# One TensorE signal per slot in a hand-scheduled vision tower kernel

## The reference, cut to what matters

```python
# tok: 256 patches of 16 pixels, mean, layer norm, attention over the 16 pixels
kv = _ln(unf, ln_kv_w, ln_kv_b) @ Wkv.T
h1 = reduce_feats + softmax(q * scale . k) . v @ proj_w.T + proj_b
# attn: gated scan over 256 tokens, forward and backward, 16 states
h = exp(delta * A) * h + delta * u * B ;  y = h . C + D * u
h2 = h1 + (sigmoid(gate(mean y)) * y * silu(z)) @ W_out
# ffn: product keys, 8 heads; the best 16 of 64x64 rows of a table per token and head
sim = einsum(q, pk_keys); scores, idx = top_k(sim, 16)       # twice
final_scores, pk_idx = top_k(score, 16)                      # of the 16x16 pairs
k, v = weighted sums of keys_table, values_table rows        # one per token
out = h2 + sum over heads of causal_softmax(q k^T) v @ Wo
```

## Time and profile before

| | us |
|---|---|
| median of three runs (lowest, highest) | 17585.84 (17570.04, 17600.08) |
| profiled execution: span | 17612.8 |
| one image: span / 64 | 275.2 |
| PE, ACT, DVE, POOL busy | 13397.9, 7416.4, 10470.6, 10063.1 |

### The profile page before, as it was taken

The page is one execution under the profiler, slowest core; times in us unless marked ns, Lnnn a source line. Parts: engine busy times, 40 slices in busy tenths (PEclk is TensorE's granted clock), DMA queues, the critical chain, the costliest instruction groups (busy, mean ns, idle before and its releaser), DMA issues.

```text
span 17612.8 us, 261382 instructions
## 1 busy us (share of the span) xinstructions
PE 13397.9 (76%) x71228; PEld 10390.9 (59%) x71228; DVE 10470.6 (59%) x39940; ACT 7416.4 (42%) x17286; POOL 10063.1 (57%) x9220
## 2 busy tenths in 40 slices
PE   4777777777777777777777778777777777777777
PEld 3656556556565555565656656556556665565565
DVE  6656656566566566565665656656656566566562
ACT  2444444444444444444444444444444444344443
POOL 2555555556556556555555556555655555556565
PEclk6888888888888888888888888888888788788888
DMA  2444434444444344343443444444434444344343
GB/s 80 115 114 113 114 108 115 118 110 119 114 112 118 108 115 122 107 116 109 116 117 107 118 111 120 117 113 116 116 108 117 115 112 116 105 116 122 107 116 95
DMA packets 1643030, 1984.06 MB, mean 113 GB/s; under 512 B 527806, under 2 KB 1129022, under 8 KB 1628990
## 3 DMA queue, kind: packets, MB, share of 16 engines
q1 hardware_dynamic: 1346366, 1359.69, 27.2%
q0 software_dynamic: 294912, 604.57, 13.2%
HBM read 1898.00 MB, written 65.01 MB: 111 GB/s over the span
## 4 chain that ended last, share of the span: by engine, by line
PE 38%; another core or an unknown queue 20%; DVE 15%; issue 13%; ACT 8%; DMA 4%; SPq 1%; DVEq 0%; ACTq 0%
PE bank L890 9%; PE bank L926 6%; DMA moving<-keyspace 4%; PE bank L913 4%; ACT bank L1158 3%; PE bank L907 3%; PE bank L767 2%; PE bank L814 2%; PE bank L875 2%; ACT weight L1164 2%; PE bank L896 1%; PE bank L949 1%; PE bank L851 1%; DVE decay L1484 1%
## 5 line engine op out<-in xcount | busy, mean ns | idle before, releaser
L695 POOL DMA_INDIRECT gath<-in_table_dram,rowsT x9216 | 10062.9, 1092 | 7503.4 <-PE bank L926 3775.8
L890 PE MATMUL bank<-weight,rowtab 128*128 128x256 f32 x12288 | 3919.7, 450 | 0.0
L1164 ACT ACTIVATE weight<-bank 128x512 f32<-128x512 f32 x3584 | 2129.3, 594 | 2782.6 <-PE bank L913 1536.2
L890 PEld LDWEIGHTS bank<-weight,rowtab 128*128 128x128 f32 x12288 | 2814.0, 230 | 825.2 <-issue 196.6
L926 PEld LDWEIGHTS bank<-spread,gath 128*128 128x128 f32 x18432 | 2868.0, 223 | 202.3 <-issue 14.5
L913 PE MATMUL bank<-moving,pick_b 96*128 96x512 bf16 x3584 | 1583.5, 442 | 1730.9 <-ACT bank L1158 1282.0
L926 PE MATMUL bank<-spread,gath 128*128 128x96 f32 x18432 | 2773.9, 301 | 15.6 <-issue 15.3
L1158 ACT ACTIVATE bank<-bank,seventeen 128x512 f32<-128x512 f32 x3584 | 2379.1, 664 | 545.9 <-issue 408.5
L907 PE MATMUL bank<-moving,pick_b 96*128 96x512 bf16 x3584 | 1590.2, 444 | 420.4 <-DMA moving<-keyspace 256.4
L913 PEld LDWEIGHTS bank<-moving,pick_b 96*128 96x128 bf16 x3584 | 400.9, 112 | 2268.3 <-ACT bank L1158 1545.6
L1731 DVE TENSOR_REDUCE negmax<-bank 128x1 f32<-128x128 f32 x512 | 147.8, 289 | 2601.6 <-remote 1389.4
(11 more groups left out here) (266 smaller groups left out, 20279.7 us busy)
## 6 DMA issues: line engine op xcount, KB each, us to landing
rowtab<-in_tableD_dram SPq DMA_DIRECT2D x2048, 256.0 KB
wide<-states SPq DMA_DIRECT2D x512, 512.0 KB
moving<-keyspace SPq DMA_DIRECT2D x3072, 64.0 KB
gath<-in_table_dram,rowsT POOLq DMA_INDIRECT x9216
moving<-keyspace SPq DMA_DIRECT2D x3072, 32.0 KB
pix<-in_x_dram SPq DMA_DIRECT2D x64, 1024.0 KB
pix<-in_x_dram SPq DMA_DIRECT2D x128, 512.0 KB
keyspace<-split SPq DMA_DIRECT2D x192, 256.0 KB, 2.0
```

Source lines behind the costliest of these rows:

```text
L695: pool.indirect_dma_start(out=gath[:, u % RING, j, :], out_offset=None, in_=table, in_offset=bass.IndirectOffsetOnAxis(ap=rowsT[k][:, col: ...
L890: last = mm(dense_ps[:, 0:TOK], rowtab[:, r, s % 2 * 2 + half, :], weight[s % 2][:, half * TOK:(half + 1) * TOK], start=(s % 16 == 0 and h ...
L1164: af(weight[s % 2][:], zd_ps[s % 2][:], ACT.Exp, scale=-1.0).then_inc(weight_ready, 1)
```

## The change

Of TensorE's steps only `o` still signals once per slot (`slot_step`), beside the steps of tok and of the lists that keep their own semaphore (kv, rf, t0 to t2, q, pj, xz, dt, xd, tb, s0 to s3). Everything else, z, d, g, all stages of attention, A, E, y, g of the gate and bk, signals nothing. A reader waits until slot_step has counted the first `o` that stands behind the step it reads (`seen`). An image had 285 signals of TensorE: 56 each of z, o and d, 36 of g, 40 of attention, 12 of kv, 12 others of FIRST, 17 of SECOND. Now it has 82: 56 of o, 12 of kv, 9 others of FIRST, 5 of SECOND.

The order is now written out per engine, slot by slot. Readers of the moved signals stand one slot later (ScalarE's qT from row 7 to row 8, for example). Stages 0 and 2 of attention are one step, whose two results ScalarE copies one behind the other. Stage 6 stands before `o`, and `d` stands before `o` in four of the 56 slots. The eight steps e0 to e7 are four (E0 to E3), each of both halves, and their eight copies four. What is computed is the same.

Shortened diff:

```diff
-1 a.sq3                                  (tables by slot, all engines)
+PE_ORDER = """
+0 z55-1 a5.6-1 o0+0 d54-1 a6.0-1
+7 z6+0 a6.6-1 o7+0 d5+0 a7.0-1 S.tb+1 F.kv3+2 F.kv4+2
...
+def stands(text):
...
+    for row in text.split("\n"):
+        slot, *todo = row.split() or ("",)
+        at = [t[0] for t in todo].index("o") if todo else 0
+        for i, t in enumerate(todo):
+            where[t[:-2]] = int(slot) - int(t[-2:]) * SLOTS + (1 if i <= at else 2)
...
+        def seen(b, name):
+            return (b + LEAD) * SLOTS + place[name]
...
             def overs(b, s):
...
-                   skip_group_check=True).then_inc(over_mm, 1)
+                   skip_group_check=True).then_inc(slot_step, 1)
...
             def exponents(b, s):
...
-                   skip_group_check=True).then_inc(z_ready, 1)
+                   skip_group_check=True)
...
             def load_keys(b, k, s):
-                wait(sp, z_ready, b * SLOTS + s - KEY_RING + 1)
+                if s >= KEY_RING:
+                    wait(sp, slot_step, seen(b, f"z{s - KEY_RING}"))
...
             def gather_image(b, k):
-                    wait(pool, summed, b * PARTS + (u - RING + 1))
+                    if u >= RING:
+                        wait(pool, slot_step, seen(b, part_name(u - RING)))
...
             def weights(b, s):
-                act.wait_ge(z_ready, b * SLOTS + s + 1)
-                wait(act, dense_done, b * SLOTS + s - 1)
+                act.wait_ge(slot_step, seen(b, f"z{s}"))
+                if s >= 2:
+                    wait(act, slot_step, seen(b, f"d{s - 2}"))
...
             def attention(...):                       (TensorE)
                 if stage == 0:
                     wait(pe, acc_ready, n)
...
+                    if h <= DENSE:
+                        pe.wait_ge(kept, a * (DENSE + 1) + (h + 1))
...
-                if stage == 2:
-                    pe.wait_ge(qT_copied, n + 1)
...
-                        last = mm(att_ps[:, 256 + t * C:256 + (t + 1) * C], kvh[C:P, t * P:(t + 1) * P],
-                                  wo_ffn[C:P, h, :], start=True, stop=True)
-                    last.then_inc(vo_ready, 1)
+                        mm(att_ps[:, 384 + t * C:384 + (t + 1) * C], kvh[C:P, t * P:(t + 1) * P],
+                           wo_ffn[C:P, h, :], start=True, stop=True)
```

More of the change, by code:

```diff
@@ new lines @@
+"""
+SP_ORDER = """
+0 t2+0 m3+0
+1 st2+0 m4+0
+2 t3+0 m5+0
+3 m6+0
+4 t4+0 m7+0
+5 m8+0
+6 st3+0 t5+0 m9+0
+7 m10+0
+8 t6+0 m11+0
+9 m12+0
+10 t7+0 m13+0
+11 m14+0
+12 t8+0 m15+0
+13 x+3 m16+0
+14 t9+0 m17+0
+15 m18+0
+16 t10+0 m19+0
+17 out-1 m20+0
+18 t11+0 m21+0
+19 m22+0
+20 t12+0 m23+0
+21 m24+0
+22 t13+0 m25+0
+23 m26+0
+24 t14+0 m27+0
+25 m28+0
+26 t15+0 m29+0
+27 m30+0
+28 t16+0 m31+0
+29 m32+0
+30 t17+0 m33+0
+31 m34+0
+32 t18+0 m35+0
+33 m36+0
+34 t19+0 m37+0
+35 bc+2 m38+0
+36 t20+0 m39+0
@@ L680, in _ @@
+            for b in range(-LEAD, 3):
+                period(b, b % 2)
+            with sp.Fori(0, (IMAGES - 6) // 2) as i:
+                period(i * 2 + 3, 1)
+                period(i * 2 + 4, 0)
+            for b in range(IMAGES - 3, IMAGES + 1):
+                period(b, b % 2)
             sp.wait_ge(stored, 16 * IMAGES)
```

750 lines of the change are left out of this document (391 added, 359 removed).

## The result

| | before | after |
|---|---|---|
| median of 4 runs, us | 17577.94 | 17445.26 |
| lowest, highest | 17549.95, 17600.08 | 17397.62, 17454.19 |
| profiled execution: span | 17612.8 | 17395.6 |

The ratio is 0.9919, 95% interval 0.9896 to 0.9942: 0.8% faster, 133 us, where 4.5% was forecast. The time falls outside the forecast's own range and stands within 50 us of where rival (2) put it, 17495 us.

The account below looks back on a forecast made before the run. No engine was full; late TensorE signals and waits behind them were taken as the limit. Gains 620 + 230 + 500 + 190 = 1540 us, costs 744 us, less 27 us to the median: 17612.8 to 16790 us, range 16250 to 17350.

Parts of the forecast that it names:

- rival (2): Lateness of TensorE's signals has nothing to do with their number, only the readers' order helps: 17495 us, 0.5% faster; chance 10%.
- First term, queueing: Moved readers on ScalarE no longer hold w and l behind a late signal, so TensorE waits less before z: 620 us gained.
- Second term, returned results: TensorE's idle time before a head's stage 0 and the one-hot matmuls, 459 us, falls as steps merge: 230 us gained.
- Third term, the number: With 203 of 285 TensorE signals an image gone, a fifth of the possible 2509 us of lateness goes: 500 us gained.
- Fourth term, the clock: Less idle time on TensorE turns some half-clock time to full clock: 190 us gained, half of 380 us.
- The costs: Added waits in the new order, on w, d, stage 6, probT's copy and stage 0: 744 us lost in sum.
- w's wait for o: ScalarE's exponential w waits for o behind z, 0.22 us later, where z waits for ScalarE: 304 us lost.
- Stage 6 ahead of o: TensorE's stage 6 before o delays w, 162 us lost; its wait for probT's copy loses another 138 us.
- Stage 0 (51 us): TensorE's stage 0 follows stage 6 within one slot and may wait for VectorE's additions: 51 us lost, at most 512.
- GpSimd's wait: GpSimd's waits end up to a slot later, hidden by the ring of six parts and loads ahead: cost put at nothing.
- rival (1): Lateness goes with the number of TensorE's signals, so the third term is 2509 us: 15441 us in all; chance 15%.
- Rival (3): The slot's loop z, o, w, l gets longer and becomes the bound, waiting on o's signal: 18259 us; chance 29%.

## Why the prediction was wrong

**The condition of the signals.** The prediction read rightly from the earlier trace rows that the signals are late while GpSimd gathers. It then took lateness for something that fewer signals and other readers would ease. The runs show no such easing: lateness costs the kernel before 17348.45 - 14326.07 = 3022 us and the changed one 17235.07 - 13854.69 = 3380 us. The change is worth 471 us without it and 113 us with it, 358 us less. That is about half of what is missing from the forecast's gain of 17586 - 16790 = 796 us; for the other half the forecast was too high even for prompt signals.

**First term, queueing (620 us).** The sign is shown, the size is off. The place of attention's readers alone is worth 227 us in the late condition. The mis-sized step is "72% of z's 1731 us, of which half": idle time before z fell by 119 us. The copies' waits did vanish, but w's wait for the slot's signal grew in their place (2783 to 7442 us), because the signal ahead of which they had waited was the late one.

**Second term, returned results (230 us).** Failed. The idle time before stage 0 and the one-hot sums went from 459 to 896.6 + 205.1 = 1102 us.

**Third term, the number (500 us).** Failed, and this is the step that was only argued ("a fifth"). All 203 signals back cost 31 ± 49 us where signals are late, and the signal of o is as late with 82 signals as with 285 (1.3 us on the mean). The lower end, nothing, was right.

**Fourth term, the clock (190 us).** Failed in the first measurement: the clock rose by 0.004 and TensorE's busy time grew by 62 us. Where signals are prompt it fell by 150 us (12049.3 to 11899.1).

**The costs (744 us).** Partly refuted, partly untested. w's wait for o (304 us) stays open, since the run meant to undo it left that wait in 51 of 56 slots. Stage 6 ahead of o and its wait for probT (162 + 138 us): undone, the kernel is 0.6% slower where signals are prompt, and TensorE is idle for only 5.5 us before stage 6 where they are late. d ahead of o (89 us) was not tried alone. Stage 0 (51 us): its idle time is 655 us more than before, over the bound of 512, yet it decides little, since taking 601 us of it away gave 120 us, VectorE's additions included. GpSimd's wait was put at nothing, on the ground that the ring hides it. That term failed: in the late condition the wait for the slot's signal is worth 416 us as a gain, more than any other part that was measured.

So the gains of 1540 us were far too large, and so was the difference from the costs. With late signals the slot's loop waits for one signal whose delay goes with the gathers. The runs fit idle times before single steps that are shares of one wait and not a sum of independent ones: with 601 us taken away before stage 0, 811 came back before z and the one-hot sums.

**Rival (2)** has the mechanism nearest to what happened: lateness does not depend on the number. Its signs came too, the unknown part stays and the kv copies still wait (947.7 and 733.5 us). That its 17495 us is so near is partly luck, since it is a difference of gains (835 us) and costs (744 us) of which neither was found in that size, and GpSimd's part is missing from it. It had 10%., two signals 4 us apart both late, had spoken for it and against rival (1). Rival (3)'s first sign, a growing wait before z, did not come, nor did idle time before stage 6. Stage 0's did, and so did its mechanism in part: w, l, z and GpSimd all wait for the one late signal. The point from which it would decide was misjudged. By its own terms costs pass gains when w's delay tells in (950 - 440) / 1183 = 43% of the slots, not in two thirds, and the 39% of the earlier trace rows stand near that.

## What to carry to other kernels

Before pricing a late wait, ask what makes it late: if the cause (here another engine's gathers) stays, moving or removing waits moves the idle time to the next step, and a sum over idle groups counts the same wait many times. Fewer semaphore signals were worth nothing measurable here. Readers that stand a slot later were worth 1.3% where signals are late, and a later wait of GpSimd 2.4%. When a step is undone to price it, look for a second wait that still holds it. Measure a kernel at different times: its own time moved by 21% on one chip, and the worth of the change between 3.4 and 0.6%.

## What the runs showed of the hardware

Two conditions of one program: 14326.07 and 17336.38 us for the kernel before, on one chip in two sessions. Prompt sessions were the first three (14318.37, 14307.49 and 14326.07 us), late ones the last three and the first measurement. In the late one TensorE's signals can come whole microseconds late while GpSimd's indirect gathers run (5.0 us in the timeline above), in the prompt one 0.03 to 0.04 us after the matmul with the same gathers. Over the whole trace of the kernel before, 43% of the recorded arrivals of TensorE's signals are over 0.3 us late: 54% of those whose matmul ends while gathers run, and 13% of the others. VectorE's signals come late too, 10% of them in the kernel before and 16% in the changed one; ScalarE's under 1%. In the prompt condition it is 0.1 to 0.2% for TensorE and 0.1% for VectorE. With a quarter of the gathers the changed kernel takes 13645 us in either condition. What differs between the conditions, and why a gather delays TensorE's signals at all, was not found; whether each matmul that ends adds to the delay (theory M) could not be told, since the kernel with d cut in two met the prompt condition.
